# Mixer B's chunk loop: the state product on plain C, its result multiplied by decay rows that come through DRAM, and another order of gates and residuals

## The reference

```python
xBC = silu(causal_conv(xBC) + conv_b)          # 4 taps
xs, Bm, Cm = split(xBC)                        # xs: 4 heads of 64, Bm and Cm: 128 states
dt = softplus(dt + dt_bias); A = -exp(A_log)   # one per head
h = h * exp(dt_t * A) + dt_t * x_t B_t         # per head, 64 x 128
y_t = h C_t                                    # then y + D * xs
y = rmsnorm(y * silu(z), ssm_norm_w) @ out_proj_w.T
```

## Time and profile before

| | us |
|---|---|
| median of 3 runs (lowest, highest) | 998.67 (996.67, 999.59) |
| the profiled execution: device time | 1006.71 |
| the profiled execution: span of its profile | 1004.4 |
| busy in the span: PE, PEld | 957.7 (95%), 678.4 (68%) |
| busy in the span: DVE, ACT, POOL | 722.4 (72%), 568.1 (57%), 616.2 (61%) |

### The profile page before, as it was taken

How to read it: one execution, slowest core, us unless ns; L and a number is a source line. 1 busy time by engine, 2 the same in 40 slices (tenths; PEclk the granted TensorE clock), 3 DMA queues, 4 the chain that set the end, 5 groups by cost and what they waited for, 6 DMA issues and landing times. The chain is left out here.

```text
span 1004.4 us, 16126 instructions
## 1 busy us (share of the span) xinstructions
PE 957.7 (95%) x4711; PEld 678.4 (68%) x4711; DVE 722.4 (72%) x1192; ACT 568.1 (57%) x1046; POOL 616.2 (61%) x482
## 2 busy tenths in 40 slices
PE   7999999898899998999999999999999999999997
PEld 3323333232366797999999556667666999999996
DVE  3999998999678665566665697776597666666665
ACT  6664655655442554555554698787733555555553
POOL 1599897999630967854642378963305777667432
PEclk9899979999999999999999999999999999999999
DMA  5323223363250233222000400000702222411104
GB/s 157 66 73 86 74 76 74 85 108 94 87 158 26 62 87 94 75 73 76 28 33 17 119 24 1 2 1 1 224 0 71 66 79 62 131 62 39 33 24 132
DMA packets 69247, 69.70 MB, mean 69 GB/s; under 512 B 14952, under 2 KB 51568, under 8 KB 69168
## 3 DMA queue, kind: packets, MB, share of 16 engines
q1 hardware_dynamic: 64176, 58.44, 20.6%
q0 software_dynamic: 4992, 10.23, 3.9%
HBM read 58.00 MB, written 10.62 MB: 68 GB/s over the span
## 5 line engine op out<-in xcount | busy, mean ns | idle before, releaser
L810 POOL TENSOR_TENSOR a_hc<-a_h,a_c_sb 128x512 f32<-128x512 f32 x128 | 159.4, 1267 | 49.1 <-DVE a_h L711 48.9
L492 PE MATMUL ps<-a_hc,eye 128*128 128x512 f32 x256 | 135.2, 642 | 12.9 <-POOL a_hc L810 12.2
L629 ACT ACTIVATE ps<-a_delta,a_neg_a 128x512 f32<-128x512 f32 x128 | 87.0, 689 | 72.2 <-DVE a_h L711 70.5
L492 PEld LDWEIGHTS ps<-a_hc,eye 128*128 128x128 f32 x256 | 45.5, 196 | 82.6 <-POOL a_hc L810 42.2
L711 DVE TENSOR_TENSOR_SCAN a_h<-ps,a_state,a_b_u 128x512 f32<-128x512 f32 x64 | 78.7, 1266 | 1.6 <-POOL a_hc L810 0.8
L1214 PE MATMUL ps<-f_ring_rounded,f_q_hi_rounded 128*128 x312 | 77.0, 337 | 1.3 <-DVE f_q_hi_rounded L1746 1.3
L1214 PE MATMUL ps<-g_ring_rounded,g_q_hi_rounded 128*128 x312 | 77.1, 337 | 0.1
L711 DVE TENSOR_TENSOR_SCAN a_h<-ps,a_b_u 128x512 f32<-128x512 f32 x64 | 75.1, 1207 | 2.8 <-ACT ps L629 2.7
L1067 POOL DMA_INDIRECT g_rows<-xn_rows,g_source x39 | 37.2, 954 | 56.1 <-DVE g_source L1700 35.4
L1067 POOL DMA_INDIRECT f_rows<-xn_rows,f_source x39 | 37.3, 956 | 52.9 <-DVE f_source L1700 35.5
L691 DVE TENSOR_TENSOR a_b_u<-a_du,ps 128x1024 f32<-128x1024 f32 x57 | 68.1, 1195 | 1.6 <-PE ps L479 1.5
(11 more groups left out here) (486 smaller groups left out, 2740.3 us busy)
## 6 DMA issues: line engine op xcount, KB each, us to landing
a_c_sb<-c_rows SPq DMA_DIRECT2D x64, 256.0 KB, 3.4
f_ring<-in_gu SPq DMA_DIRECT2D x16, 469.0 KB
g_ring<-in_gu SPq DMA_DIRECT2D x16, 469.0 KB
f_ring<-in_dn SPq DMA_DIRECT2D x8, 512.0 KB
g_ring<-in_dn SPq DMA_DIRECT2D x8, 512.0 KB
xn_rows<-f_work SPq DMA_DIRECT2D x8, 256.0 KB, 4.0
f_rows<-token_rows SPq DMA_DIRECT2D x8, 256.0 KB, 4.6
xn_rows<-g_work SPq DMA_DIRECT2D x8, 256.0 KB, 4.0
```

The source lines that it names most:

```text
L492: nc.tensor.matmul(ps[:, Y + f, :], k.eye[:, :], hc[:, s % WAITING, :], start=False, stop=(n == NST - 1)).then_inc(y_added, 1)
L629: nc.scalar.activation(ps[:, A + m % NA, :], delta[:, f, cols(g)], ACT.Exp, scale=neg_a[:, f, n:n + 1])\
L810: nc.gpsimd.tensor_tensor(hc[:, m % WAITING, :], h[:, s % DEPTH, :], c_sb[:, i % RING, :], ALU.mult)\
```

## The change

The state's product is taken with plain C, for two heads at a time, into a bank of its own (`INTER`, the bank that E had). What C was multiplied by, exp(E), is multiplied onto the result instead (`take_inter`, DVE). For that the decays must lie one head-half per 64 partitions: they are computed once, ahead of the loop, as a 64x128 tile (`decays_of`, one matmul and one exp), written to DRAM, and read back broadcast, for four chunks at a time, two loads of 64 partitions each, into `shifted`. `gate_y` gets one more DVE step, which adds this part to Y. E, its exp and `c_in` are gone. The first chunk of each sequence has no state, so that its product, its `keep` and its zeroed state go too. In chunks 3, 5, 8 and 9 (`WHOLE_STEPS`) the steps are one fp32 product on POOL and one fp32 matmul on PE, in place of a high and a low part. DVE's gates stand at even c (2 to 12, and 13) instead of at 2, 3, 6, 7, 10, 11 and 13; the first two residuals stand at 7 and 11 instead of 6 and 10; PE's `variance` follows `chunk_outputs` instead of preceding it. The order on ACT and POOL is not edited otherwise.

```diff
+            sp.wait_ge(rows_ready, 1)
+            sp.dma_start(k.decay_rows, decays_of[:, :]).then_inc(rows_moved, 16)
+            sp.wait_ge(rows_moved, 16)
+            half = HEADS * TT // 2
+            for g in range(NCH):
+                if g == 0:
+                    sp.wait_ge(pool_conv, 2 * (TAPS - 1))
+                else:
+                    sp.wait_ge(rows_moved, 16 + 32 * g)
+                if g >= 2:
+                    sp.wait_ge(inter_read, (g - 1) * GROUP // PAIR)
+                for q in range(2):
+                    rows = k.decay_rows[q * half:(q + 1) * half, :].rearrange("(f t) m -> f (t m)", f=FT)
+                    sp.dma_start(of_decays(g)[q * HD:(q + 1) * HD, :, :], rows[:, cols(g)].partition_broadcast(HD))\
+                        .then_inc(rows_moved, 16)
...
+                nc.tensor.matmul(ps[0:n, M, 2 * n:2 * n + P], dta[:, :, :, :].rearrange("p q f t -> p (q f t)"),
+                                 k.masks[:, 0, :], start=True, stop=True).then_inc(ends_ready, 1)
...
+                if c in WHOLE_STEPS:
+                    return nc.tensor.matmul(out, k.masks[:, 1, :], steps_whole[:, c % 2, :, :].rearrange("p h i -> p (h i)"),
+                                            start=True, stop=True)
...
-                if c >= 1:
-                    pe.wait_ge(c_in_ready, c)
-                of_steps(ps[:, E, :], one[:, :], c).then_inc(e_ready, 1)
...
-                pe.wait_ge(c_in_ready, c + 1)
-                pe.wait_ge(state_ready, c + 1)
                 for h in range(HEADS):
                     a = h // 2 * PAIR * P + c % PAIR * P
-                    out = ps[HD * (h % 2):HD * (h % 2) + HD, Y + g % 2, a:a + P]
-                    nc.tensor.matmul(out, x_dt[:, c % 2, h, :], mix[:, c % 2, h, :], start=True, stop=False)
-                    last = nc.tensor.matmul(out, state[:, c % 2, h, :], c_in[:, c % 2, h, :], start=False, stop=True)
+                    last = nc.tensor.matmul(ps[HD * (h % 2):HD * (h % 2) + HD, Y + g % 2, a:a + P], x_dt[:, c % 2, h, :],
+                                            mix[:, c % 2, h, :], start=True, stop=True)
+                if c % PER_SEQ:
+                    pe.wait_ge(state_ready, states_of(c))
+                    if g:
+                        pe.wait_ge(inter_read, g)
+                    for f in range(FT):
+                        a = f * PAIR * P + c % PAIR * P
+                        last = nc.tensor.matmul(ps[:, INTER, a:a + P],
+                                                state[:, c % 2, 2 * f:2 * f + 2, :].rearrange("p h q -> p (h q)"),
+                                                cT[:, c * P:(c + 1) * P], start=True, stop=True)
...
+                chunk_outputs(c)
                 if c in (8, 12):
                     variance(c // 4 - 2)
-                chunk_outputs(c)
...
-                act.wait_ge(e_ready, c + 1)
-                nc.scalar.activation(ps[:, E, :], ps[:, E, :], ACT.Exp).then_inc(into_ready, 1)
...
+            nc.scalar.activation(decays_of[:, :], ps[0:n, M, 2 * n:2 * n + P], ACT.Exp).then_inc(rows_ready, 1)
             for c in range(TT):
                 chunk(c)
-                if c % PER_SEQ:
+                if c % PER_SEQ > 1:
                     keep(c - 1)
...
-                dve.wait_ge(into_ready, c + 1)
-                nc.vector.tensor_tensor(c_in[:, c % 2, :, :], ps[:, E, :].rearrange("p (h i) -> p h i", h=HEADS),
-                                        cT[:, ts].unsqueeze(1).to_broadcast([P, HEADS, P]), ALU.mult)\
-                    .then_inc(c_in_ready, 1)
...
+            def take_inter(g):
+                dve.wait_ge(y_summed, PAIR * (g + 1))
+                n = g * PAIR // GROUP
+                dve.wait_ge(rows_moved, 16 + 32 * (n + 1))
+                a = g * PAIR % GROUP * P
+                decay = of_decays(n)[:, :, a:a + PAIR * P].rearrange("p f (c m) -> p f c m", c=PAIR)
+                nc.vector.tensor_tensor(chunks_of(from_state, g), chunks_of(in_pair(INTER), g), chunks_of(decay, g), ALU.mult)\
+                    .then_inc(inter_read, 1)
...
-                dve.wait_ge(yd_ready, (g + 1) * FT)
+                dve.wait_ge(inter_read, g + 1)
+                dve.wait_ge(yd_ready, g * (FT + 1) + FT)
+                y_now = chunks_of(in_pair(Y + g % 2), g)
+                nc.vector.tensor_tensor(y_now, y_now, chunks_of(from_state, g), ALU.add).then_inc(yd_ready, 1)
+                dve.wait_ge(yd_ready, (g + 1) * (FT + 1))
...
                     prepare(c + 1)
                     next_state(c + 1)
-                if c in (2, 6, 10):
+                if c % PAIR:
+                    take_inter(c // PAIR)
+                if c % PAIR == 0 and 0 < c < 14:
                     gate_y(c // PAIR - 1)
-                if c in (6, 10, 14):
+                if c in (7, 11, 14):
                     residual(c // 4 - 1)
-                if c in (3, 7, 11, 13):
+                if c == 13:
                     gate_y(c // PAIR)
```

More of the change, by code:

```diff
@@ L37 @@
 TT = T // P
+HEADS_B = 4
 TILES = NI + 1
@@ L1888, in mixer_b_stage @@
     shifted = sb("shifted", [P, 2, SEQ])
-    dt, dt_log, dta, dt_end, e_end = [sb(n, [P, TT, HEADS]) for n in "dt dt_log dta dt_end e_end".split()]
+    dt, dt_log, dt_end, e_end = [sb(n, [P, TT, HEADS]) for n in "dt dt_log dt_end e_end".split()]
+    dta = sb("dta", [P, 2, FT, TT])
+    dta_by_head = dta[:, :, :, :].rearrange("p q f t -> p t f q")
     dta_hi, dta_lo = [sb(n, [P, TT, HEADS], F32R) for n in ("dta_hi", "dta_lo")]
@@ L1892, in mixer_b_stage @@
     one, later = [sb(n, [P, P], F32R) for n in ("one", "later")]
-    steps_hi, steps_lo = [sb(n, [P, 2, HEADS, P], F32R) for n in ("steps_hi", "steps_lo")]
+    steps_whole, steps_hi = k.twin("b_steps_hi", [P, 2, HEADS, P], stage)
+    steps_lo = sb("steps_lo", [P, 2, HEADS, P], F32R)
     toks = sb("toks", [P, 2, 3 * P])
     gram = sb("gram", [P, 2, P])
-    mix, c_in = [sb(n, [P, 2, HEADS, P]) for n in ("mix", "c_in")]
+    mix = sb("mix", [P, 2, HEADS, P])
+    decays_of = sb("decays_of", [HEADS * TT, P])
+    from_state = sb("from_state", [P, FT, 2, P])
     x_dt, x_end, state = [sb(n, [P, 2, HEADS, HD]) for n in ("x_dt", "x_end", "state")]
@@ L1927, in mixer_b_stage @@
     ROT = 4
-    Y, S, M, D, F, E, TR = 0, 2, 3, 4, 5, 6, 7
+    Y, S, M, D, F, INTER, TR = 0, 2, 3, 4, 5, 6, 7
+    WHOLE_STEPS = (3, 5, 8, 9)
+    GROUP = CH // P
     G, O = 4, 0
@@ L1974, in part_of_x, with of_decays, chunks_of, in_pair @@
         return x_split[:, part, cols(c)]
+    def of_decays(g):
+        return shifted[:, g % 2, :].rearrange("p (f t) -> p f t", f=FT)
+    def chunks_of(v, g):
+        return v[:, :, (1 if 2 * g % PER_SEQ == 0 else 0):, :]
+    def in_pair(bank):
+        return ps[:, bank, :].rearrange("p (f c m) -> p f c m", f=FT, c=PAIR)
+    def steps_of(c):
+        return sum(1 if n in WHOLE_STEPS else 2 for n in range(c + 1))
+    def states_of(c):
+        return sum(1 for n in range(c + 1) if n % PER_SEQ)
+    def kept_of(c):
+        return sum(1 for n in range(c + 1) if n % PER_SEQ > 1)
     def p_at(part, q):
@@ L2046, in ends, with of_steps @@
                                      start=False, stop=True).then_inc(ends_ready, 1)
-            def of_steps(out, which, c):
-                nc.tensor.matmul(out, which, steps_hi[:, c % 2, :, :].rearrange("p h i -> p (h i)"),
+                n = HEADS * TT
+                nc.tensor.matmul(ps[0:n, M, 2 * n:2 * n + P], dta[:, :, :, :].rearrange("p q f t -> p (q f t)"),
+                                 k.masks[:, 0, :], start=True, stop=True).then_inc(ends_ready, 1)
+            def of_steps(out, c):
+                if c in WHOLE_STEPS:
+                    return nc.tensor.matmul(out, k.masks[:, 1, :], steps_whole[:, c % 2, :, :].rearrange("p h i -> p (h i)"),
+                                            start=True, stop=True)
+                nc.tensor.matmul(out, later[:, :], steps_hi[:, c % 2, :, :].rearrange("p h i -> p (h i)"),
                                  start=True, stop=False)
-                return nc.tensor.matmul(out, which, steps_lo[:, c % 2, :, :].rearrange("p h i -> p (h i)"),
+                return nc.tensor.matmul(out, later[:, :], steps_lo[:, c % 2, :, :].rearrange("p h i -> p (h i)"),
                                         start=False, stop=True)
@@ L2065, in chunk_inputs @@
                     pe.wait_ge(mix_ready, c)
-                of_steps(ps[:, D, :], later[:, :], c).then_inc(d_ready, 1)
+                of_steps(ps[:, D, :], c).then_inc(d_ready, 1)
                 if c >= 1:
@@ L2369, in _ @@
             nc.scalar.preload_act_table_set(LOG_EXP)
[L2370 to L2373, removed]
+            act.wait_ge(ends_ready, 3)
+            n = TT * HEADS
+            nc.scalar.activation(flat(e_end), ps[:, M, 0:n], ACT.Exp).then_inc(ends_done, 1)
+            nc.scalar.activation(flat(dt_end), ps[:, M, n:2 * n], ACT.Exp).then_inc(ends_done, 1)
```

(7 more changed lines are left out.)

43 lines of the change are left out of this document (28 added, 15 removed).

## The result

The changed kernel takes 1011.19 us (median; 1007.82 to 1012.05) against 999.02 for the kernel before on the same chip: ratio 1.0123, 95% interval 1.0104 to 1.0143, 12.2 us slower. The sign was right, the size (+6.2) was half of it, and the time lies outside the range of 999.0 to 1008.5.

What follows compares the result with a forecast made beforehand. PE was taken to set the loop's pace, ACT's in-order queue close behind. Stretches of -3.0, +2.2, +3.4, -0.8, +3.6 and +0.8 summed to +6.2 on 998.67: 1004.8 us, range 999.0 to 1008.5.

Steps and rivals of the forecast that it cites:

- three late squares: ACT's squares 0, 1, 2 wait for moved gates, delaying mix(6), mix(10), mix(14): +2.2 (states 5 to 9), +3.4, +3.6.
- states 6 to 9, 10 to 13 and 14 to the last gate: Loop stretches behind the stalls, priced from DVE's work and waits at 12.5, 12.3 and 8.4 us.
- the loop's start: From loop's start to state(5): 19.05 us before, 16.1 after, so -3.0.
- DVE's balance: In the loop, take_inter and the additions to Y cost DVE 9.5, c_in's removal saves 9.6: busy time stays about 49.
- a pair: Two steady-state chunks cost DVE 6.2 us, 3.1 per chunk, against PE's earlier pace of 3.19.
- That relief: PE's loop work: 10.6 us less of its 60.38, from E, the outputs and the whole steps.
- The rule I had set against the trace: Weight loads' busy share (69%), not matmuls' 98%, shows PE's nearness to its limit; so relieving PE would give little.
- My bound: Four output records with plain C cost between 0 and S's 0.70, S taken as twice the columns; 0.44 chosen.
- DVE's 49.3: DVE's busy time in the loop after the change, also taken as its limit under the faster rival.
- the rival of the late rows: Decay rows land late, take_inter(0) waits up to 3 us: 1007.8; chance 0.08.
- the relief: Rival: PE's 10.6 less is gained in most chunks, squares' waits cost half, loop about 57.5: 994.5; chance 0.14.
- the cancelling: Rival: stalls as forecast but half as long, about +1: 999.7, within 0.3%; chance 0.16.

Runs made afterwards that it cites:

- e1: Kernel before with only the changed order: gates at even chunks, two residuals one chunk later, variance behind the outputs; 1010.11 us, ratio 1.0109 to the kernel before.
- e5: Changed kernel, even gates kept, with the whole chain behind them (squares, mean squares, projection and so on) one chunk later; 997.21 us, ratio 0.9987 to the kernel before.
- e3: Changed kernel with ten small useless matmuls on TensorE during its wait for each of the first three mean squares; 1006.43 us, ratio 1.0084 to the kernel before.
- e9: Kernel before with its old state product, but even gates and the whole chain behind them one chunk later; 1003.36 us, ratio 1.0007 to the kernel before.
- e7: Changed kernel with gates, residuals and variance at their old places and without the whole steps; 1000.53 us, ratio 1.0017 to the kernel before.
- e4: Changed kernel with the residuals back at chunks 6, 10 and 14, gates left even; 1006.47 us, ratio 1.0080 to the kernel before.
- e2: Changed kernel with gates, residuals and variance back at their old places, new state product kept; 999.44 us, ratio 1.0014 to the kernel before.
- e8: Changed kernel with TensorE filled during its waits for the mean squares and the residuals back at their old places; 1005.12 us, ratio 1.0085 to the kernel before.
- e6: Changed kernel with the old order and 17 idle 128x128 matmuls in TensorE's pauses at the loop's start; 1001.13 us, ratio 1.0022 to the kernel before.
- e10: Changed kernel with the chain behind the gates one chunk later, plus 16 idle matmuls ahead of the loop-end variance; 1002.32 us, ratio 1.0011 to the kernel before.

## Why the prediction was half right

**The order, right.** For the three late squares the forecast's mechanism, place and price held: 6.9 for states 9 to 10 and 13 to 14 (measured 6.98, 7.00), 5.7 for 5 to 6 (5.76), 2.5 and 1.3 of wait (2.65, 1.41), squares 0.7 behind the gate (0.72). e1 and e5 show it from both sides.

**The step that failed: PE's records taken at their old lengths** in the stretches behind the stalls. I saw that PE would have gaps, wrote "PE with gaps in every chunk", and then priced states 6 to 9, 10 to 13 and 14 to the last gate as if it came out of them at the same speed: the clock was a term that the sum put at nothing, without a reason. e3, at full clock there, measures my sum's own terms, and the changed kernel what was missing:

| stretch | forecast | e3 | after | before |
|---|---|---|---|---|
| states 6 to 9 | 12.5 | 12.8 | 13.8 | 13.3 |
| states 10 to 13 | 12.3 | 12.4 | 15.5 | 13.1 |
| state 14 to last gate | 8.4 | 8.5 | 9.0 | 7.6 |
| state 5 to last gate | 52.7 | 53.5 | 58.0 | 43.5 |

Of the 6.0 that were missing (12.2 - 6.2) the clock is 4.5 (58.0 - 53.5), the waits' own underestimate 0.8 (53.5 - 52.7), and 0.7 the loop's start: -2.3 instead of -3.0 up to state(5). The MLP did shift as a whole (from the last gate to the load 35.84, before 35.87).

**DVE's balance, right, a pair too cheap.** DVE is busy 50.50 in e5 up to the last gate, 51.06 before; PE 55.65 against 61.30, at a mean granted clock of 0.99. That relief is 5.7, where I had 10.6 (a term that the sum didn't use), and it was worth 2.55 up to the last gate (e9 against e5, the whole steps included): DVE and its waits take over. A full pair between stalls took 7.0 in e5 (states 9 to 11: 3.97 + 3.02), not 6.2, with a wait of 0.67 for exp(10) and one of 0.39 for keep in it. The pair of states 2 to 4, whose products are halved, took 6.8 in the trace after, where my pitches give 5.6 (2 x 1.66 + 0.33 + 0.91 + 0.45 + 0.61); 0.53 of it is the wait for the decay rows and 0.38 one for S. The rule I had set against the trace (the Trainium skill, "Perfetto Trace Analysis", section "Identifying the Most-Contended Engine") read the loop better than PE's 98% did.

**Smaller terms.** The outputs went from 1.08 to 1.13 (608.51 - 607.38 in the trace after), where I had 0.98: the four records of 128x128 with plain C cost 0.55 (608.51 - 607.96), as much as the eight that they replace. My bound had misread the rows: S is two records of 256 columns, which is as many columns as four of 128, and not twice as many. DVE's 49.3 should have been 49.2 (49.56 - 0.1 - 0.3). A whole step cost little, as far as e7 tells. The rows' loads took 4.4 (page, DMA issues) instead of 3.4:

```profile
b_shifted<-decay_rows SPq DMA_DIRECT2D x8, 256.0 KB, 4.4
```

I had forecast no wait of DVE for them. There is one, at the first `take_inter`, 0.38 to 0.56 in the six traces that have it:

```profile
607.12 0.42 DVE L2664 TENSOR_TENSOR b_from_state<-ps,b_shifted 128x256 f32<-128x256 f32 x1 [0.53 <-DMA b_shifted<-decay_rows]
```

That is far from the 3 of the rival of the late rows, which fell with it; the relief and the cancelling fell with e1.

## What to carry to other kernels

When an instruction moves by one place, list who waits for it on the in-order engines, and move that whole chain by one as well: here the same gates cost 11 to 12 us with the squares left where they were (e1) and nothing with the chain moved (e5, e9). A stall of TensorE is priced twice: the wait, and what runs at the lower clock behind it, if TensorE is what the others then wait for. Before paying for the relief of the busiest engine, add up the next engine with its hand-overs, not its busy time alone.

## What the runs showed of the hardware

The granted clock fell to 1.2 GHz behind single waits of TensorE, and not behind each. It fell behind waits of 2.68, 2.63 and 3.11 us in the changed kernel, of 2.09 and 2.11 in e1, of 2.69 and 1.84 in e4, and behind one of 1.89 in e5 that followed a wait of 1.02. It did not fall behind 1.80 in e4, 1.67 in e9 and 1.38 in e1. Behind pauses of 1.1 and 0.40 at the loop's start it fell in four executions (e2, e3, e4, e8) and stayed in four others. The length of the one wait doesn't settle it: 1.80 and 1.84, in one execution, went different ways, and what decides between them stays open. Ten idle matmuls of 128x128 in the wait kept it up, three times of three in e3. The Trainium skill, "TensorE: Matmul & The Clock Gate", section "HAM oscillation — how this bites in real kernels", tells of the same fall when TensorE waits for DMA in each round of a loop; here a wait for another engine's square did it, three times in a loop that is otherwise dense, for 4.5 us. Filling has a price of its own: one such fp32 matmul took 0.23 us, and with more than twice as many as the pause held (17 instead of 7 in e6, 16 instead of 7 in e10) the next real work came 0.9 and 1.5 us later, which gave back most of what the clock gained.
